# Feed-forward products of a four-layer kernel: one plain fp32 matmul on unsplit operands in place of three fp32r matmuls on high and low parts

## The reference, cut to what matters

```python
        mi = rms_norm(hidden_states, ln_post_attn_w)
        v_out = jax.nn.silu(mi @ v_gate) * (mi @ v_up) @ v_down
        l_out = jax.nn.silu(mi @ l_gate) * (mi @ l_up) @ l_down
        hidden_states = hidden_states + jnp.where(vm, v_out, l_out)
...
        h = layernorm(x, ln_ff_g, ln_ff_b)
        h = jax.nn.gelu(h @ W1, approximate=False) @ W2
        x = x + jnp.tanh(ff_gate) * h
```

## Time and profile before

| what | value |
|---|---|
| median of 3 runs | 2504.32 us (2503.06 to 2508.76) |
| the profiled execution's own time | 2509.57 us |
| its span in the trace | 2507.8 us |
| mean granted TensorE clock | 0.96 |
| PE busy | 2311.2 us, 92% of the span |
| PEld busy | 1890.0 us, 75% |
| DVE busy | 1410.7 us, 56% |
| ACT busy | 1143.7 us, 46% |
| POOL busy | 653.1 us, 26% |

### The profile page before, as it was taken

How to read it: one execution, slowest core, us unless ns; L and a number is a source line. 1 busy time by engine, 2 the same in 40 slices (tenths; PEclk the granted TensorE clock), 3 DMA queues, 4 the chain that set the end, 5 groups by cost and what they waited for, 6 DMA issues and landing times. The chain is left out here.

```text
span 2507.8 us, 63604 instructions
## 1 busy us (share of the span) xinstructions
PE 2311.2 (92%) x24286; PEld 1890.0 (75%) x24287; DVE 1410.7 (56%) x2866; ACT 1143.7 (46%) x2585; POOL 653.1 (26%) x833
## 2 busy tenths in 40 slices
PE   5994999997996999799999997998999998997998
PEld 4673788875765999688888876996888875666998
DVE  3563666664775333466666655554666665764433
ACT  2553444443664333334344344445444435664332
POOL 1333222212662222111111110001222214652222
PEclk9996999997998999899999998998999998998999
DMA  5440000002003111300000001000000002001111
GB/s 179 58 58 9 18 15 15 15 15 71 27 27 93 55 58 57 110 2 2 2 2 2 2 2 35 0 0 14 15 15 15 15 13 79 27 30 51 59 59 42
DMA packets 78468, 85.55 MB, mean 34 GB/s; under 512 B 19891, under 2 KB 69376, under 8 KB 78112
## 3 DMA queue, kind: packets, MB, share of 16 engines
q1 hardware_dynamic: 56016, 41.55, 7.3%
q10 hardware_dynamic: 13856, 19.61, 2.4%
q0 software_dynamic: 8368, 21.15, 2.4%
HBM read 52.22 MB, written 21.40 MB: 29 GB/s over the span
## 5 line engine op out<-in xcount | busy, mean ns | idle before, releaser
L1184 POOL TENSOR_TENSOR s_kx<-s_qkt,const 128x512 f32<-128x512 f32 x128 | 131.7, 1049 | 447.3 <-ACT s_qkt L1115 447.3
L2150 PE MATMUL ps_all<-f_wh,f_xh 128*128 x396 | 155.2, 392 | 10.6 <-DVE f_xl L2295 10.6
L1536 POOL TENSOR_TENSOR c_kx<-c_qkt,const 128x512 f32<-128x512 f32 x128 | 130.5, 1037 | 118.2 <-ACT c_qkt L1480 118.0
L534 POOL TENSOR_TENSOR a_probs<-a_probs,a_sm 128x1024 f32<-128x1024 f32 x32 | 60.9, 1902 | 384.6 <-DVE a_sm L529 384.6
L1123 ACT ACTIVATE s_pt<-ps_all 128x512 f32<-128x512 f32 x128 | 69.7, 594 | 186.9 <-PE ps_all L1005 186.9
L2151 PE MATMUL ps_all<-f_wh,f_xl 128*128 x396 | 149.3, 377 | 0.0
L2152 PE MATMUL ps_all<-f_wl,f_xh 128*128 x396 | 149.2, 377 | 0.0
L1874 ACT ACTIVATE self_w<-ps_all,a_q_bias 128x256 f32<-128x256 f32 x128 | 53.7, 470 | 196.5 <-PE ps_all L1722 196.5
L2290 DVE SCALAR_TENSOR_TENSOR f_h<-ps_all,rstd,f_act_g 128x688 f32<-128x688 f32 x66 | 61.6, 934 | 143.9 <-PE ps_all L2152 131.9
L2175 PE MATMUL ps_all<-f_dh,f_hh 128*128 x396 | 116.9, 295 | 4.0 <-DVE f_hl L2305 4.0
L505 DVE TENSOR_REDUCE s_mx<-ps_all 128x8 f32<-128x512 f32 x128 | 82.5, 686 | 61.3 <-PE ps_all L991 61.3
(11 more groups left out here) (322 smaller groups left out, 7518.7 us busy)
## 6 DMA issues: line engine op xcount, KB each, us to landing
s_v_swap<-s_v_own SPq DMA_DIRECT2D x128, 68.0 KB, 2.0
f_x_in<-x_sorted SPq DMA_DIRECT2D x66, 128.0 KB, 2.0
x_res<-x_sorted SPq DMA_DIRECT2D x66, 128.0 KB, 2.1
x_sorted<-x_res POOLq DMA_DIRECT2D x1, 4224.0 KB, 16.5
l_rows<-in_x SPq DMA_DIRECT2D x32, 128.0 KB, 3.6
x_res<-in_x SPq DMA_DIRECT2D x32, 128.0 KB, 7.4
x_res<-x_back SPq DMA_DIRECT2D x1, 3584.0 KB, 20.5
l_rows<-in_ctx SPq DMA_DIRECT2D x32, 64.0 KB, 4.3
```

The lines of the kernel that those rows point to most:

```text
L1184: ins = nc.gpsimd.tensor_tensor(kx[:, p % 2, c], qkt[:, p % 2, 2 + c].rearrange("p (b k) -> p b k", b=2).unsqueeze(2) .broadcast_to([P, 2, ...
L1536: ins = nc.gpsimd.tensor_tensor(kx[:, p % 2, b], qkt[:, p % 2, 1, b * S:b * S + S].unsqueeze(1).broadcast_to([P, RH, S]), const[:, C_H8X:C ...
L2150: nc.tensor.matmul(bank, x_high, wh[:, w_at], start=(c == 0), stop=False)
```

## The change

Both feed-forwards lose their high and low tiles. Gated: `wg` (all gate and up weights times the norm weight) and `wd` (down weights, padded) are plain fp32; ACT writes expert "v"'s half of `wd` and the gate parts of `wg`, DVE the up parts and expert "l"'s half, side by side instead of one after the other. x and h are copied once, by ACT (`x_copy`, `h_copy`), into `xt` and `ht`; the DVE subtractions go. Gelu: the loaded weights are used as they are, without any preparation; ACT's Gelu writes `h` directly, and the copy and the subtraction go. Each product is one matmul call on fp32 tiles. Order of steps, tiles, banks, transposes and transfers stay.

```diff
-                wh = ob("wh", [P, 2 * CH * GU], F32R)
-                wl = ob("wl", [P, 2 * CH * GU], F32R)
-                dh = ob("dh", [P, 2 * IC * D], F32R)
-                dl = ob("dl", [P, 2 * IC * D], F32R)
+                wg = ob("wg", [P, 2 * CH * GU])
+                wd = ob("wd", [P, 2 * IC * D])
                 x_in = ob("x_in", [P, 2, D])
-                xh = ob("xh", [P, CH * P], F32R)
-                xl = ob("xl", [P, CH * P], F32R)
+                xt = ob("xt", [P, CH * P])
                 act_g = ob("act_g", [P, 2, I])
...
-                hl = ob("hl", [P, IC * P], F32R)
+                ht = ob("ht", [P, IC * P])
                 junk = ob("junk", [P, D])
                 down_banks = (ps_o, ps_d)
...
                                 for c in range(CH):
-                                    w_at = bass.ds(at + (c * GU + lo), n)
-                                    x_high, x_low = xh[:, c * P:c * P + P], xl[:, c * P:c * P + P]
-                                    nc.tensor.matmul(bank, x_high, wh[:, w_at], start=(c == 0), stop=False)
-                                    nc.tensor.matmul(bank, x_low, wh[:, w_at], start=False, stop=False)
-                                    ins = nc.tensor.matmul(bank, x_high, wl[:, w_at], start=False, stop=(c == CH - 1))
+                                    ins = nc.tensor.matmul(ps_gu[:, lo:lo + n], xt[:, c * P:c * P + P],
+                                                           wg[:, bass.ds(at + (c * GU + lo), n)],
+                                                           start=(c == 0), stop=(c == CH - 1))
                                 if b > 0:
                                     ins.then_inc(gu_pe.handle, 1)
 
...
-                                w_at = bass.ds(at + m * D, D)
-                                high, low = hh[:, m * P:m * P + P], hl[:, m * P:m * P + P]
-                                nc.tensor.matmul(bank, high, dh[:, w_at], start=(m == 0), stop=False)
-                                nc.tensor.matmul(bank, low, dh[:, w_at], start=False, stop=False)
-                                ins = nc.tensor.matmul(bank, high, dl[:, w_at], start=False, stop=(m == IC - 1))
+                                ins = nc.tensor.matmul(bank, ht[:, m * P:m * P + P], wd[:, bass.ds(at + m * D, D)],
+                                                       start=(m == 0), stop=(m == IC - 1))
                             ins.then_inc(d_pe.handle, 1)
...
-                        pe.wait_ge(wlow_ok.handle, wlow_ok.at(4 * CH))
+                        pe.wait_ge(whigh_ok.handle, whigh_ok.at(2 * CH))
+                        pe.wait_ge(wlow_ok.handle, wlow_ok.at(2 * CH))
...
-                            for r in range(2):
-                                at = (2 * k + r) * I
-                                nc.scalar.activation(wh[:, at:at + I], w_in[:, k, r], ACT.Copy,
-                                                     scale=w_ln[:, k % CH:k % CH + 1]).then_inc(whigh_ok.handle, 1)
+                            at = 2 * k * I
+                            nc.scalar.activation(wg[:, at:at + I], w_in[:, k, 0], ACT.Copy,
+                                                 scale=w_ln[:, k % CH:k % CH + 1]).then_inc(whigh_ok.handle, 1)
...
-                        for e in range(2):
-                            at = e * IC * D
-                            nc.scalar.activation(dh[:, at:at + full * D],
-                                                 w_down[:, e, 0:full].rearrange("p c n -> p (c n)"), ACT.Copy) \
-                                .then_inc(whigh_ok.handle, 1)
-                            nc.scalar.activation(dh[0:last, at + full * D:at + IC * D], w_down[0:last, e, full], ACT.Copy) \
-                                .then_inc(whigh_ok.handle, 1)
-                        act.wait_ge(wlow_ok.handle, wlow_ok.at(4 * CH + 4))
+                        nc.scalar.activation(wd[:, 0:full * D], w_down[:, 0, 0:full].rearrange("p c n -> p (c n)"), ACT.Copy) \
+                            .then_inc(whigh_ok.handle, 1)
+                        nc.scalar.activation(wd[0:last, full * D:IC * D], w_down[0:last, 0, full], ACT.Copy) \
+                            .then_inc(whigh_ok.handle, 1)
+                        act.wait_ge(wlow_ok.handle, wlow_ok.at(2 * CH + 2))
+                        act.wait_ge(whigh_ok.handle, whigh_ok.at(2 * CH + 2))
                         load_next(act)
                         tile_steps(act, step)
...
-                            if has_tile(t + 1):
-                                x_low(t + 1)
                             if has_tile(t - 1):
                                 residual(t - 1, 1 - u)
-                            if has_tile(t):
-                                h_low(t)
+                        dve.wait_ge(loaded.handle, loaded.at(0, 144))
...
+                            at = (2 * k + 1) * I
+                            nc.vector.tensor_scalar(wg[:, at:at + I], w_in[:, k, 1], w_ln[:, k % CH:k % CH + 1], None, ALU.mult) \
+                                .then_inc(wlow_ok.handle, 1)
                         dve.wait_ge(hpad_ok.handle, hpad_ok.at(1))
...
+                        at = IC * D
+                        nc.vector.tensor_copy(wd[:, at:at + full * D], w_down[:, 1, 0:full].rearrange("p c n -> p (c n)")) \
+                            .then_inc(wlow_ok.handle, 1)
+                        nc.vector.tensor_copy(wd[0:last, at + full * D:at + IC * D], w_down[0:last, 1, full]) \
+                            .then_inc(wlow_ok.handle, 1)
...
+                xt = ob("xt", [P, CH, GT])
+                h = ob("h", [P, M, GT])
...
-                                    at = c * FF + m * P
-                                    high, low = wh[:, at:at + P], wl[:, at:at + P]
-                                    nc.tensor.matmul(in_banks[m % 4], high, xh[:, c], start=(c == 0), stop=False)
-                                    nc.tensor.matmul(in_banks[m % 4], high, xl[:, c], start=False, stop=False)
-                                    ins = nc.tensor.matmul(in_banks[m % 4], low, xh[:, c], start=False,
-                                                           stop=(c == CH - 1))
+                                    ins = nc.tensor.matmul(in_banks[m % 4], w_in[:, c, m * P:m * P + P], xt[:, c],
+                                                           start=(c == 0), stop=(c == CH - 1))
                                 ins.then_inc(g_pe.handle, 1)
...
                                     if i == 0:
-                                        pe.wait_ge(h_ok.handle, h_ok.at(g * M + (m + 1)))
-                                    high, low = hh[:, m, i * P:i * P + P], hl[:, m, i * P:i * P + P]
-                                    nc.tensor.matmul(bank, high, oh[:, m * D:m * D + D], start=(m == 0), stop=False)
-                                    nc.tensor.matmul(bank, high, ol[:, m * D:m * D + D], start=False, stop=False)
-                                    ins = nc.tensor.matmul(bank, low, oh[:, m * D:m * D + D], start=False,
-                                                           stop=(m == M - 1))
+                                        pe.wait_ge(a_ok.handle, a_ok.at(g * M + (m + 1)))
+                                    ins = nc.tensor.matmul(bank, h[:, m, i * P:i * P + P], w_out[:, m],
+                                                           start=(m == 0), stop=(m == M - 1))
...
-                        pe.wait_ge(wlow_ok.handle, wlow_ok.at(2 * CH))
...
-                                if h_ok.due(g * M + (m - 1)):
-                                    act.wait_ge(h_ok.handle, h_ok.at(g * M + (m - 1)))
-                                nc.scalar.activation(h[:, m % 2], in_banks[m % 4], ACT.Gelu).then_inc(a_ok.handle, 1)
-                                act.wait_ge(a_ok.handle, a_ok.at(g * M + (m + 1)))
-                                if d_pe.due(g * G):
+                                if m == 0 and d_pe.due(g * G):
                                     act.wait_ge(d_pe.handle, d_pe.at(g * G))
-                                nc.scalar.activation(hh[:, m], h[:, m % 2], ACT.Copy).then_inc(hhigh_ok.handle, 1)
+                                nc.scalar.activation(h[:, m], in_banks[m % 4], ACT.Gelu).then_inc(a_ok.handle, 1)
...
-                        for high, _, w, at in splits[:2 * CH]:
-                            nc.scalar.activation(high[:, at:at + HALF], w[:, at:at + HALF], ACT.Copy) \
-                                .then_inc(whigh_ok.handle, 1)
                         xt_copy(0)
-                        for high, _, w, at in splits[2 * CH:]:
-                            nc.scalar.activation(high[:, at:at + HALF], w[:, at:at + HALF], ACT.Copy) \
-                                .then_inc(whigh_ok.handle, 1)
...
-                                dve.wait_ge(hhigh_ok.handle, hhigh_ok.at(g * M + (m + 1)))
-                                nc.vector.tensor_tensor(hl[:, m], h[:, m % 2], hh[:, m].bitcast(F32), ALU.subtract) \
```

(58 more changed lines are left out.)

55 lines of the change are left out of this document (15 added, 40 removed).

## The result

The kernel with plain fp32 products takes 2614.88 us (median of 4 runs, 2613.52 to 2617.49), against 2505.38 (2503.06 to 2508.76) before it on the same chip: ratio 1.0437, 95% interval 1.0419 to 1.0455, 109.5 us slower. The profiled execution took 2614.39 us, span 2612.6.

A forecast was written before the change was run, and what follows sets the result against it. PE's matmul stream was taken to bound the three changed phases. Products +89.0 and +41.0, less starts and ends of 6.4, 3.7, 2.7 and 2.0, gave +115.2 us: median 2619.5, rounded 2620 us, range 2602 to 2650.

The forecast's parts named there:

- What bounds: Gated and gelu phases: PE's matmul stream is the bound, ACT and DVE split work hidden except at starts and ends.
- The price of a plain call: Plain fp32 matmuls: two records a call, 0.216, 0.296 and 0.429 us each at 256, 352 and 512 columns.
- The 0.48 rival: Gated and gelu products: 512-column records step at 0.48 us, +40 us, 2660 us in all; chance 6%.
- the one of 0.104 for each call: Rival for gated and gelu products: every call, not every burst, pays 0.104 us extra; +109, 2729 us; chance 2%.
- one pass pair a call: Rival for gated and gelu products: a plain call costs one pass pair, not two; about 2262 us, faster; chance 3%.
- Gated products, +89.0: Gated gate_up and down: tile from 6.75 to 8.13 us over 66 tiles, first gate_up of each phase excluded, +89.0 us.
- Gelu products, +41.0: Gelu phase products: a group from 22.4 to 27.55 us, +5.13 for each of 8 groups, +41.0 us.
- Starts and ends, -14.8: Gated starts in layers 1 and 3, gelu start, gated ends: -6.4, -3.7, -2.7 and -2.0 us from less preparation and waiting.
- layer 1: Start of layer 1's gated phase: halved copies let ACT reach `load_next` 6.4 us earlier, at 783.2; -6.4 us.
- Layer 3: Start of layer 3's gated phase: PE starts 4.35 us earlier, its first records slower at the low clock; -3.7 us.
- Gelu's wait: Start of the gelu phase: PE starts behind ACT's copy instead of waiting for the last low part; -2.7 us.
- Ends: Ends of both gated phases: about half of the last down's 1.98 us wait, the subtraction of h, goes; -2.0 us.

The follow-up runs named there:

- e4: Kernel before, gated phases with the changed kernel's preparation and three identical fp32r calls a product, gelu unchanged: 2494.28 us against 2506.98, 0.9951.
- e1: Kernel before with plain fp32 products in the two gated phases only, gelu unchanged: 2579.01 us against 2506.98, 1.0287.
- e6: Kernel before with the gated down product in two halves of 128 columns: 2638.5 us against 2509.18, 1.0521.
- e7: Changed kernel with the gated down product in two halves of 128 columns: 2624.48 us against 2509.18 for the kernel before, 1.0465.
- e3: Kernel before with two of the three fp32r matmuls of each product, all splits kept: 2385.43 us against 2509.18, 0.9512.
- e10: e3 with the weight offset fixed at 0 in the gated phases, no register in addresses: 2356.39 us, 0.9394 of the kernel before.
- e5: e4 with one fp32r matmul a gated product instead of three: 2336.57 us against 2509.18 for the kernel before, 0.9317.
- e9: e5 with the weight offset fixed at 0, no register in addresses: 2305.04 us against 2508.18 for the kernel before, 0.9190.
- e11: Kernel before with the weight offset fixed at 0 in the gated phases, no register in addresses: 2507.06 us, 1.0002.
- e8: Kernel before with `load_next` issued by SP and ACT's Silu table loaded early by a one-column activation: 2500.16 us against 2506.98, 0.9974.

## Why the prediction was right

- **What bounds.** Right. In the gated phases the split work of DVE and ACT lay wholly behind PE (e4: tile 6.75 with half of it gone), and PE had no slack that would have hidden the price (220.00 of 220.00 us busy). For gelu no run takes the split work away with the products kept; there the trace of the kernel before shows it, PE busy 23.44 of the 23.44 us of a group.
- **The price of a plain call.** Right, from layer 0's rows and the durations' growth: 0.216, 0.296 and 0.429 a record were forecast; 0.216, 0.296 and 0.429 to 0.430 were measured, two records a product. The 0.48 rival and the one of 0.104 for each call are out, and so is one pass pair a call.
- **Gated products, +89.0.** Mis-sized by a little: 84.7 measured (e1 less e4, with the slower first `gate_up` of each phase in it, which the forecast had put to the starts). The tile is 8.085 in place of 8.13: 0.045 x 66 = 3.0 us too much. That it came so near is partly luck. The term put 0.104 us on the first record of each burst, from a record behind a wait, and left the transposes as they were. In the middle of the phase no burst pays that: 4.62 and 2.59 us are the bare 8 x 0.429 + 4 x 0.296 and 12 x 0.216. But the eight transposes of a tile take 0.88 us in place of 0.71, and the two errors (0.208 too much, 0.17 too little) nearly cancel.
- **Gelu products, +41.0.** The group went from 23.44 to 28.42, +4.98 in place of +5.13: 8 x 0.15 = 1.2 us too much. The term took the bare products on both sides; the transposes and the change from one kind of call to the other come to 23.44 - 22.4 = 1.0 us before and 28.42 - 27.55 = 0.87 now.
- **Starts and ends, -14.8.** Together right, with errors inside that cancel. e4 (gated only) gives -12.7 against the -12.1 forecast for the gated phases. In layer 1 `load_next` came 5.7 us earlier behind ACT's first copy and not 6.4: ACT's small work took 1.6 us in place of 0.96 (and the term's own parts add up to 783.07, not 783.2). From the first PE transpose to the second `gate_up` it is 12.7 us in place of 19.4, -6.7; the tile behind it took 9.80 (granted clock 0.83) in place of 7.87 (0.84), which is 0.6 more than the new tile period explains. Layer 3: 11.2 in place of 15.57, -4.3 (forecast -3.7), and the tile behind it took 8.18 us at 1.00 in place of 8.06 at 0.82, a gain of 1.2 us that the forecast doesn't have. Gelu's wait 3.56 to 0.87, -2.7 (-2.7). Ends: 1.98 to 0.98, -2.0 for both (-2.0).
- **Rule against rows.** The four passes of the Trainium skill (FP8 and Floating Point Precision, TensorE Precision Notes) agree with the trace as a count: 0.429 us is twice what 512 columns take at one a cycle, and there are two such records. As a price against three fp32r passes they overstate, 173 us to the some 124 measured for the products (109.5 with the starts' 14.8), since fp32r calls step at 0.227 to 0.232 and not at 0.213.

The terms of the products were 3.0 + 1.2 = 4.2 us too large, of the 5.7 between the forecast +115.2 and the measured +109.5. The remaining 1.5 is less than the interval of the comparison can tell.

## What to carry to other kernels

Price a matmul by the distance between starts times the number of records, never by a row's length: here 0.39 us rows started every 0.23, and adding up lengths would have given the wrong sign. When the matmul engine is busy throughout a phase, vector and activation work taken away buys only its start and its end, as e4 shows for the gated phases. Those ends are worth a look on their own, since issuing DMAs from an idle engine, with the table load brought forward, gave 6.8 us without touching the arithmetic. The choice between one plain fp32 product and three fp32r products depends on the width of the output: at 256 and 512 columns three fp32r calls were cheaper, at 128 the plain one was.

## What was not expected of the hardware

- **A fp32r call has a floor.** 128 columns step at 0.112 us (e6) against 0.119 for 256; plain records come down to the same 0.112 at 128 columns, which is near half of their 0.216 (e7). A fixed hand-over on top of the columns' time, which 0.119 and 0.232 suggest, is refuted by e6; a floor fits. Whether the load of the 128x128 weights sets it was not measured by itself.
- **Register-addressed matmuls cost PE's sequencer.** With bursts cut to 12 or 6 fp32r calls, loading and computing the offsets left holes of 0.25 to 0.51 us and made the whole kernel 29 to 32 us longer (e3 to e10, e5 to e9). With 18 calls a burst they cost nothing (e11: 1.0002), and the changed kernel's 6 longer plain calls leave no hole either.
- **The tile behind a wait can be dearer than the wait says.** In the kernel before it ran at a granted clock of 0.84 and 0.82 in layers 1 and 3, in e8 with its shorter waits at 1.00, which is 1.1 and 1.3 us less. What decides it stays open: in layer 3 of the changed kernel it ran at 1.00 behind the old wait of 1.91 us.
- Left open: why 512-column fp32r calls step at 0.232 in the gated phase and mostly at 0.227 in gelu (not the register, e11). It is not the phase as such: in the kernel before, the first six steps of gelu's `up` after `down` take 0.232 too (1597.54 to 1598.93), and only the later ones 0.227. Open as well is why fp32r records at 256 and 512 columns take 12 to 19 ns more than one column a cycle, while plain records there take 2 to 3 ns more than two cycles a column.
